# A delta-rule attention and expert kernel: 128 units written out with constant waits, and v brought into its bank by a transpose

## The chip, the cores and the metric

The kernel runs on one core of a Trainium2 chip. The metric is the time of one execution on the device in microseconds (us). A program on one core is timed several times; the time of before is the median of 3 runs.

## The reference, cut to what matters

The input has 4 sequences of 1024 tokens with 512 features. After a layer norm, 16 heads run a gated delta rule over time, and a mixture of experts follows. The change lies in the attention part:

```python
q = _short_conv(hidden_states @ Wq, conv_q)      # k and v likewise; silu at the end
q = _l2norm(q) * SCALE; k = _l2norm(k)
g_eff = -exp(A_log) * softplus(hidden_states @ Wf1 @ Wf2 + dt_bias)
beta = sigmoid(hidden_states @ Wb)
def step(S, inp):                                # for every token
    qt, kt, vt, gt, bt = inp
    S = S * exp(gt)[..., None]
    err = einsum('bhk,bhkv->bhv', kt, S)
    delta = bt[..., None] * (vt - err)
    S = S + kt[..., None] * delta[:, :, None, :]
    return S, einsum('bhk,bhkv->bhv', qt, S)
y = o * silu(hidden_states @ Wg + bg)            # then an RMS norm and Wo
```

## The kernel before, in words

The program has three parts. A prologue (to about 250 us) normalises x, transposes it into `xT`, and stores `beta` and the decays to scratch. The attention part (to about 5680 us) walks 128 units: 16 heads (H) times 8 chunks of 128 tokens (J), each unit holding all 4 sequences (B), 512 columns in all. The mixture (to the end) multiplies by Wo and runs the experts.

In the attention part a step works on three units at once. Unit a is being projected (q and k), convolved and normalised; unit m = a - 1 gets its table of decayed products between keys and queries in seven levels; unit b = a - 2 has its triangular system inverted in six levels and is scanned with the state. TensorE (PE), VectorE (DVE), ScalarE (ACT) and GpSimd (POOL) each have one `step` function, and the order of work in it is written out by hand. SyncE (SP) loads weights per head and `beta_u` and `decay_u` per unit. All engines meet only through semaphores, and each semaphore counts up by a fixed number per unit: `Signal.at(unit, k)` is the value that `wait` (L512) waits for.

`walk` calls `step` for each triple of units. It uses loops of the machine (`Fori`): an outer one over seven pairs of heads, in it an inner one per head over three pairs of chunks, and two steps written out at each head's end. The last two heads stand behind the outer loop and have only the inner one. Unit numbers are registers inside a loop, so that a wait's value and a DMA's address are computed by the engine's sequencer. In the last two steps of heads 14 and 15 they are constants.

What stands in a step around the seam between two steps: on PE, at the end, L839 (the state's update), L846 (transposes of keys), L852 (sums of squares of y) and L696 (transposes of the pairs); then in the next step `project(0)` (L660, 8 matmuls), `inverse_z(1)` (L708, which waits for `T_inv` from DVE), the diagonal (L672), `level(0)` (L686), `inverse_xt(1)` (L723, L727) and the first quarter of `project(1)` (L660), which waits for `gate`. On DVE: yg (L1009), the state (L1016, or a memset at a head's end, L1012), k_hat, q_hat, KR, KQ, `T_inv` (L939), then y_out (L1029). On ACT: the store of y_out (a DMA, L1178), then in the next step the table load and `gate` (L1094), `pre` (L1051), and the copies `take_t(1)` and `take_x(1)`.

In the middle of a step stands the block of the change, L805 and L806. PE brings v into bank 7 as rows of tokens, as the product of `v_u` with the identity, and adds the product of the decayed keys with the state. ACT copies the bank to `U_r` and `U_sb` (L1141, L1142). On PE `level(5)` (L686) follows directly. An f32 product of 128 columns is two passes in the trace, and an f32 transpose is one.

Of the kernel before, what the change touches and what calls it, by code (L numbers as in the profile page):

```python
# [52 lines left out]
def wait_apart(eng, sem, value, passed):  # L53

    eng.wait_ge(sem, value)
    eng.sem_inc(passed, 1)
# [44 lines left out]
def attention(nc, ctx, env):  # L101
# [7 lines left out]
    bank, ident, ones, ln_eps = env["bank"], env["ident"], env["ones"], env["ln_eps"]  # L109
# [4 lines left out]
    def sem(name):  # L114
        return ctx.enter_context(nc.semaphore(name))
# [20 lines left out]
    with ExitStack() as c0:  # L136
# [281 lines left out]
    v_u = sb("v_u", [P, UC])  # L418
# [24 lines left out]

    HEAD_LOADS = 8
    REFINEMENTS = 2
    dve_waits_passed, pool_waits_passed, sp_waits_passed = sem("dve_waits_passed"), sem("pool_waits_passed"), \
        sem("sp_waits_passed1")
    head_loaded = sem("head_loaded")
    unit_loaded = signal("unit_loaded", 32)
    y_stored = sem("y_stored")  # L450
# [24 lines left out]
    chunk_decay_ready = signal("chunk_decay_ready", 1)  # L475
# [3 lines left out]
    unit_ready = signal("unit_ready", 1)  # L479
# [29 lines left out]
    keys_scaled = signal("keys_scaled", LEVELS)  # L509

    def wait(eng, sig, unit, k):
        eng.wait_ge(sig.sem, sig.at(unit, k))  # L512

    def cols(b):
        return slice(b * P, (b + 1) * P)
# [21 lines left out]
    def walk(eng, step):  # L537


        step(Step(par_a=0, a=0, ja=0, a_first=True, odd=0))  # L540
        step(Step(par_a=0, a=1, ja=1, par_m=0, m=0, jm=0, m_first=True, odd=1))

        def head(h, par, last):
            with eng.Fori(0, J // 2 - 1) as jj:
                for odd in range(2):
                    j = eng.snap(jj * 2 + odd)
                    b = eng.snap(h * J + j)
                    step(Step(par_a=par, a=b + 2, ja=j + 2, par_m=par, m=b + 1, jm=j + 1, par_b=par, b=b, h=h, j=j, odd=odd))
            b = h * J + (J - 2) if isinstance(h, int) else eng.snap(h * J + (J - 2))
            if last:  # L550
                step(Step(par_m=par, m=b + 1, jm=J - 1, par_b=par, b=b, h=h, j=J - 2, odd=0))
                step(Step(par_b=par, b=b + 1, h=h, j=J - 1, ends=True, odd=1))
            else:
                step(Step(par_a=1 - par, a=b + 2, ja=0, a_first=True, par_m=par, m=b + 1, jm=J - 1, par_b=par, b=b, h=h,
                          j=J - 2, odd=0))
                b = b + 1 if isinstance(h, int) else eng.snap(h * J + (J - 1))
                step(Step(par_a=1 - par, a=b + 2, ja=1, par_m=1 - par, m=b + 1, jm=0, m_first=True, par_b=par, b=b, h=h,
                          j=J - 1, ends=True, odd=1))

        with eng.Fori(0, H // 2 - 1) as hp:  # L560
            for par in range(2):
                head(hp * 2 + par, par, False)
        head(H - 2, 0, False)
        head(H - 1, 1, True)

    block = ctx.enter_context(nc.Block())

    @block.sync
    def _(sp):
        def load_head(h, par):  # L570
            at = bass.ds(h * P, P)
            for m, W in enumerate((Wq, Wk, Wv, Wg)):
                sp.dma_start(weights[par][:, m, :, :], W.rearrange("(k p) n -> p k n", p=P)[:, :, at]) \
                    .then_inc(head_loaded, 16)
            for m, c in enumerate((conv_q, conv_k, conv_v)):
                sp.dma_start(taps[par][:, m, :], c[at, :]).then_inc(head_loaded, 16)
            sp.dma_start(bg_col[par][:], bg.rearrange("(c o) -> c o", o=1)[at, :]).then_inc(head_loaded, 16)

        def load_unit(h, j, odd):
            sp.dma_start(beta_u[:], beta_scratch[bass.ds(h, 1), bass.ds(j, 1), :].rearrange("a b c -> (a b) c")  # L580
                         .to_broadcast([P, UC])).then_inc(unit_loaded.sem, 16)
            rows = decay_scratch[bass.ds(h, 1), :, bass.ds(j, 1), :].rearrange("a g b c -> (a g) (b c)")
            sp.dma_start(decay_u[odd][:], rows.unsqueeze(1).to_broadcast([NG, GG, PC])).then_inc(unit_loaded.sem, 16)

        load_head(0, 0)
        load_unit(0, 0, 0)

        def buffers_free(u, first):
            wait_apart(sp, unit_ready.sem, unit_ready.at(u, 1), sp_waits_passed)
            if not first:  # L590
                wait_apart(sp, keys_scaled.sem, keys_scaled.at(u - 1, LEVELS), sp_waits_passed)
                wait_apart(sp, chunk_decay_ready.sem, chunk_decay_ready.at(u - 1, 1), sp_waits_passed)

        def head(h, par, last):
            first = isinstance(h, int) and h == 0
            start = 0
            if first:
                buffers_free(0, True)
                load_unit(0, 1, 1)
                buffers_free(1, False)  # L600
                load_unit(0, 2, 0)
                start = 1
            if start < J // 2 - 1:
                with sp.Fori(start, J // 2 - 1) as jj:
                    for odd in range(2):
                        j = sp.snap(jj * 2 + odd)
                        buffers_free(sp.snap(h * J + j), False)
                        load_unit(h, sp.snap(j + 1), 1 - odd)
            at = h * J if isinstance(h, int) else sp.snap(h * J)
            buffers_free(at + J - 2, False)  # L610
            load_unit(h, J - 1, 1)
            if not last:
                buffers_free(at + J - 1, False)
                load_unit(h + 1, 0, 0)

        def load_next(h, par):

            wait(sp, gate_ready, h * J - 1, 1)
            wait(sp, v_conv_steps, h * J - 1, TAPS - 1)
            load_head(h + 1, 1 - par)  # L620


        sp.wait_ge(head_loaded, 16 * HEAD_LOADS)
        load_head(1, 1)
        head(0, 0, False)
        with sp.Fori(0, H // 2 - 1) as hp:
            load_next(hp * 2 + 1, 1)
            head(hp * 2 + 1, 1, False)
            load_next(hp * 2 + 2, 0)
            head(hp * 2 + 2, 0, False)  # L630
        head(H - 1, 1, True)

    @block.tensor
    def _(pe):
        def step(s):
            a, m, b = s.a, s.m, s.b
# [163 lines left out]
            if b is not None:  # L800

                wait(pe, v_silu_ready, b, 1)
                wait(pe, scan_ready, b, 1)
                for i in range(B):
                    nc.tensor.matmul(bank[7][:, cols(i)], v_u[:, cols(i)], ident[:], start=True, stop=False)  # L805
                    last = nc.tensor.matmul(bank[7][:, cols(i)], KQ_scan[:, 0, cols(i)], state[:, cols(i)], start=False,  # L806
                                            stop=True)
                last.then_inc(u_done.sem, 1)
            level(5)
            inverse_xt(6)  # L810
# [813 lines left out]
```

## Time and profile before

| | us |
|---|---|
| median of 3 runs | 6507.95 (6507.94 to 6509.31) |
| the profiled execution | 6503.2 |
| its span, first to last instruction | 6501.5 |
| PE busy | 6114.4 |
| VectorE busy | 4381.3 |
| ScalarE busy | 2961.9 |
| GpSimd busy | 1768.7 |
| mean granted TensorE clock | 0.984 |

The page gives each engine's busy time and share. The timeline gives single instructions in order of time, neighbours of one line merged, with the idle time of the engine before them and what ended it in square brackets. "<-issue" is idle time in which the engine waited for nothing that the profile shows. PEld is PE's weight load and overlaps PE. Times count from the span's start.

### The profile page before, as it was taken

Reading aid. Unit: us, or ns where it says so; the run is one execution under the profiler, and the core shown is the slowest. Engines: PE = TensorE matmul, PEld = TensorE weight load, DVE = VectorE, ACT = ScalarE, POOL = GpSimd, SP = SyncE. Lnnn points to the kernel's source line nnn. Section 1 sums busy time; section 2 is a strip of 40 time slices with the busy share of each in tenths; the row PEclk is TensorE's granted clock in tenths of the full one; section 3 lists DMA queues with packets and bytes.
Section 4 is the critical chain, followed back from the end, with each engine's and each line's share of the span. In section 5 each row is a group of like instructions: output and inputs, shape, how many; then the busy total and the mean of one; then the engine's idle time right before and its main releaser. Section 6 shows DMA issues by size and latency. Waiting matters only on the chain. (4 is left out here: it accounts for less than half of the span.)

```text
span 6501.5 us, 107897 instructions
## 1 busy us (share of the span) xinstructions
PE 6114.4 (94%) x33720; PEld 4295.4 (66%) x33720; DVE 4381.3 (67%) x7563; ACT 2961.9 (46%) x5130; POOL 1768.7 (27%) x1636
## 2 busy tenths in 40 slices
PE   5699999999999999999999999999999999899999
PEld 2477777777777767776777777767777777644444
DVE  7677777777777777777777777777777777511110
ACT  2355545555555555554555555555555555401101
POOL 2233333333333333332333333333333333200000
PEclk8899999999999999999999999999999999899999
DMA  2101010101010110101010101000111100032221
GB/s 71 45 26 30 23 34 26 33 26 31 23 33 26 33 27 20 33 26 34 26 33 20 33 26 33 26 27 26 33 26 33 26 26 26 18 117 79 83 80 44
DMA packets 183586, 234.15 MB, mean 36 GB/s; under 512 B 25048, under 2 KB 128088, under 8 KB 179168
## 3 DMA queue, kind: packets, MB, share of 16 engines
q1 hardware_dynamic: 111072, 188.22, 9.9%
q10 hardware_dynamic: 72192, 41.95, 2.2%
q8 instruction: 164, 2.69, 0.2%
q14 instruction: 158, 1.29, 0.1%
HBM read 183.75 MB, written 46.38 MB: 35 GB/s over the span
## 5 line engine op out<-in xcount | busy, mean ns | idle before, releaser
L660 PE MATMUL bank<-xT,weights 128*128 (+1 forms) x4096 | 2176.9, 629 | 83.4 <-DMA bg_col<-in_L_attn_bg 34.2
L1196 POOL TENSOR_TENSOR KR<-KR,decay_u 128x256 f32<-128x256 f32 x896 | 920.2, 1027 | 2335.2 <-PE bank L686 2335.2
L903 DVE TENSOR_TENSOR KQ<-KQ,decay_u 128x512 f32<-128x512 f32 x896 | 626.0, 699 | 857.9 <-PE bank L686 857.7
L686 PEld LDWEIGHTS bank<-KQ,KR 128*128 128x128 f32 x7168 | 918.0, 191 | 248.8 <-issue 216.7
L888 DVE SCALAR_TENSOR_TENSOR conv<-pre,taps,conv 128x512 f32<-128x512 f32 x1152 | 917.1, 796 | 124.3 <-ACT conv L1067 110.7
L686 PE MATMUL bank<-KQ,KR 128*128 128x128 f32 x7168 | 953.6, 275 | 1.1 <-DVE KQ L903 0.7
L660 PEld LDWEIGHTS bank<-xT,weights 128*128 128x128 f32 x4096 | 657.7, 193 | 294.5 <-issue 214.9
L923 DVE COPY_PREDICATED all_pairs<-level_mask,bank 128x512 f32<-128x512 int32 x896 | 796.0, 888 | 0.0
L708 PEld LDWEIGHTS bank<-T_inv,pairs 128*128 128x128 f32 x3072 | 456.9, 193 | 468.5 <-issue 247.0
L708 PE MATMUL bank<-T_inv,pairs 128*128 128x64 f32 x3072 | 654.5, 338 | 61.1 <-DVE T_inv L939 59.5
L1111 ACT ACTIVATE T_inv<-bank 128x256 fp32r<-128x256 f32 x640 | 248.9, 389 | 635.2 <-PE bank L723 635.2
L727 PE MATMUL bank<-X,ZI 128*128 128x64 f32 x3072 | 472.8, 279 | 0.0
L1378 PE MATMUL bank<-wo,y_in 128*128 128x512 f32 x1024 | 447.9, 596 | 14.2 <-DMA wo<-in_L_attn_Wo 14.2
L1094 ACT ACT_TABLE_LOAD x128 | 164.2, 1283 | 588.3 <-DVE y_out L1029 391.1
L1222 POOL TENSOR_TENSOR X<-pairs,ident_each 128x512 fp32r<-128x512 f32 x128 | 182.0, 1422 | 868.3 <-PE bank L696 868.3
L727 PEld LDWEIGHTS bank<-X,ZI 128*128 128x128 f32 x3072 | 407.0, 193 | 0.0
L723 PE MATMUL bank<-ZI,X 128*128 128x64 f32 x2560 | 396.0, 281 | 3.0 <-DVE ZI L945 3.0
L1204 POOL TENSOR_TENSOR conv<-silu 128x512 f32<-128x512 f32 x256 | 266.4, 1041 | 443.9 <-ACT silu L1076 443.9
L945 DVE TENSOR_TENSOR ZI<-bank,ident_each 128x256 fp32r<-128x256 f32 x768 | 321.5, 419 | 89.2 <-PE bank L708 88.9
L931 DVE SCALAR_TENSOR_TENSOR pairs<-bank,level_mask 128x256 fp32r<-128x256 f32 x896 | 381.4, 426 | 0.0
L1208 POOL TENSOR_TENSOR squares_rest<-conv,squares 128x512 fp32r<-128x512 f32 x256 | 360.3, 1408 | 70.2 <-POOL conv L1204 70.2
L763 PEld LDWEIGHTS bank<-delta,pairs_scan 128*128 128x128 f32 x2048 | 248.6, 191 | 181.7 <-DVE delta L964 95.8
(162 smaller groups left out, 9128.9 us busy)
## 6 DMA issues: line engine op xcount, KB each, us to landing
decay_u<-decay_scratch SPq DMA_DIRECT2D x128, 510.0 KB
beta_u<-beta_scratch SPq DMA_DIRECT2D x128, 256.0 KB
y_scratch<-y_out ACTq DMA_DIRECT2D x128, 256.0 KB, 7.0
y_in<-y_scratch SPq DMA_DIRECT2D x32, 1024.0 KB, 4.8
xt<-in_L_attn_hidden_states SPq DMA_DIRECT2D x8, 1024.0 KB, 5.3
x_in<-in_L_attn_hidden_states SPq DMA_DIRECT2D x32, 256.0 KB, 5.1
out<-o_out ACTq DMA_DIRECT2D x32, 256.0 KB, 2.0
w<-in_L_ffn_W SPq DMA_DIRECT2D x8, 704.0 KB, 4.8
```

What stands on the lines that cost most here:

```text
L660: last = nc.tensor.matmul(bank[w % 2][:], weights[par][:, w, k, :], xT[:, k, bass.ds(j * UC, UC)], start=k == 0, stop=k == KC - 1)
L686: last = nc.tensor.matmul(to[:, :, i], KR[:, cols(i)], halves(KQ[:, :, cols(i)], l, 1), start=True, stop=True)
L708: last = nc.tensor.matmul(bank[5][:, half_cols(i)], pairs[:, l, cols(i)], halves(T_inv[:, cols(i)], l, 0), start=True, stop=True)
L723: last = nc.tensor.matmul(bank[7][:, half_cols(i)], X[:, cols(i)], halves(ZI[:, l - 1, cols(i)], l, 0), start=True, stop=True)
L727: last = nc.tensor.matmul(bank[6][:, half_cols(i)], ZI[:, l - 1, cols(i)], halves(X[:, cols(i)], l, 1), start=True, stop=True)
L888: nc.vector.scalar_tensor_tensor(conv[:, w], pre[:, w, :, t:t + P], taps[par][:, w, t:t + 1], conv[:, w], ALU.mult, ALU.add).then_inc(step ...
L903: nc.vector.tensor_tensor(second_halves, second_halves, pair[:, :, 0:1].unsqueeze(1).to_broadcast([P, 2, blocks, 1 << l]), ALU.mult).then_ ...
L923: nc.vector.copy_predicated(halves(all_pairs[:], l, 1), mask.bitcast(I32).unsqueeze(1).to_broadcast([P, 2, UC >> (l + 1), 1 << l]), src)
L931: nc.vector.scalar_tensor_tensor(halves(pairs[:, l], l, 1), src[:, 0], 1.0 / GRAIN, mask, ALU.mult, ALU.mult).then_inc(pairs_ready.sem, 1)
L1196: nc.gpsimd.tensor_tensor(first_halves, first_halves, second.to_broadcast([P, UC >> (l + 1), 1 << l]), ALU.mult).then_inc(keys_scaled.sem, 1)
L1208: nc.gpsimd.tensor_tensor(squares_rest[:, w], conv[:, w].rearrange("p b t -> p (b t)"), squares[:, w], ALU.subtract).then_inc(squares_rest ...
L1378: last = nc.tensor.matmul(bank[j % 2][:], y_in[j % 2][:, h, :], wo[:, h, :], start=h == 0, stop=h == H - 1)
```

## The change

`walk` calls `step` 130 times with plain numbers; no engine's program in the attention part has a loop, and every wait and address is a constant. SP's `buffers_free` and `head` become one list in the same order of loads and waits, without the semaphore increment behind each wait (`wait_apart`); DVE and POOL keep theirs. The product of v with the identity becomes PE's transpose, all four ahead of the products with the state; only the first one of the bank starts it.

```diff
@@ walk
-        def head(h, par, last):
-            with eng.Fori(0, J // 2 - 1) as jj:
-                for odd in range(2):
-                    j = eng.snap(jj * 2 + odd)
-                    b = eng.snap(h * J + j)
-                    step(Step(par_a=par, a=b + 2, ja=j + 2, par_m=par, m=b + 1, jm=j + 1, par_b=par, b=b, h=h, j=j, odd=odd))
...
-        with eng.Fori(0, H // 2 - 1) as hp:
-            for par in range(2):
-                head(hp * 2 + par, par, False)
-        head(H - 2, 0, False)
-        head(H - 1, 1, True)
+        for a in range(H * J + 2):
+            f = dict(odd=a % 2)
+            if a < H * J:
+                f.update(a=a, ja=a % J, par_a=a // J % 2, a_first=a % J == 0)
+            if 0 <= a - 1 < H * J:
+                m = a - 1
+                f.update(m=m, jm=m % J, par_m=m // J % 2, m_first=m % J == 0)
+            if a >= 2:
+                b = a - 2
+                f.update(b=b, h=b // J, j=b % J, par_b=b // J % 2, ends=b % J == J - 1)
+            step(Step(**f))
@@ SP
-        def buffers_free(u, first):
-            wait_apart(sp, unit_ready.sem, unit_ready.at(u, 1), sp_waits_passed)
-            if not first:
-                wait_apart(sp, keys_scaled.sem, keys_scaled.at(u - 1, LEVELS), sp_waits_passed)
-                wait_apart(sp, chunk_decay_ready.sem, chunk_decay_ready.at(u - 1, 1), sp_waits_passed)
...
+        for u in range(1, H * J):
+            h, j = u // J, u % J
+            if j == 1 and 1 <= h < H - 1:
+                load_next(h, h % 2)
+            wait(sp, unit_ready, u - 1, 1)
+            if u >= 2:
+                wait(sp, keys_scaled, u - 2, LEVELS)
+                wait(sp, chunk_decay_ready, u - 2, 1)
+            load_unit(h, j, u % 2)
@@ PE, in the middle of a step
                 for i in range(B):
-                    nc.tensor.matmul(bank[7][:, cols(i)], v_u[:, cols(i)], ident[:], start=True, stop=False)
+                    nc.tensor.matmul(bank[7][:, cols(i)], v_u[:, cols(i)], ident[:], is_transpose=True, start=i == 0,
+                                     stop=False, skip_group_check=True)
+                for i in range(B):
                     last = nc.tensor.matmul(bank[7][:, cols(i)], KQ_scan[:, 0, cols(i)], state[:, cols(i)], start=False,
-                                            stop=True)
+                                            stop=True, skip_group_check=True)
                 last.then_inc(u_done.sem, 1)
```

## Rows read from the trace of the kernel before

**Rows 1.** The page: busy time and share of PE, weight loads, DVE, ACT, POOL

```profile
PE 6114.4 (94%) x33720; PEld 4295.4 (66%) x33720; DVE 4381.3 (67%) x7563; ACT 2961.9 (46%) x5130; POOL 1768.7 (27%) x1636
```

**Rows 2.** PE's timeline, L839 of units 0, 48-50, 63, 64, 118-120, 126: start, length

```profile
303.72 1.06 PE L839 MATMUL bank<-delta,k_rows 128*128 128x128 f32 x8
...
2339.74 1.06 PE L839 MATMUL bank<-delta,k_rows 128*128 128x128 f32 x8
...
2381.68 1.06 PE L839 MATMUL bank<-delta,k_rows 128*128 128x128 f32 x8
...
2423.94 1.06 PE L839 MATMUL bank<-delta,k_rows 128*128 128x128 f32 x8
...
2969.62 1.06 PE L839 MATMUL bank<-delta,k_rows 128*128 128x128 f32 x8
...
3021.10 1.06 PE L839 MATMUL bank<-delta,k_rows 128*128 128x128 f32 x8
...
5303.01 1.06 PE L839 MATMUL bank<-delta,k_rows 128*128 128x128 f32 x8
...
5344.63 1.06 PE L839 MATMUL bank<-delta,k_rows 128*128 128x128 f32 x8
...
5385.98 1.06 PE L839 MATMUL bank<-delta,k_rows 128*128 128x128 f32 x8
...
5636.90 1.06 PE L839 MATMUL bank<-delta,k_rows 128*128 128x128 f32 x8
```

**Rows 3.** The timeline, all engines, a seam inside a loop

```profile
3028.25 0.74 DVE L1029 SCALAR_TENSOR_TENSOR y_out<-yg,norm_w_col,y_rn 128x512 f32<-128x512 f32 x1
...
3029.77 1.28 ACT L1094 ACT_TABLE_LOAD   x1 [4.34 <-DVE y_out L1029]
...
3031.81 0.30 PEld L660 LDWEIGHTS bank<-xT,weights 128*128 128x128 f32 x2 [0.21 <-ACT gate L1094]
```

**Rows 4.** The timeline, all engines, the seam behind unit 118, constants on both sides

```profile
5310.13 0.73 DVE L1029 SCALAR_TENSOR_TENSOR y_out<-yg,norm_w_col,y_rn 128x512 f32<-128x512 f32 x1
...
5310.26 0.64 PE L708 MATMUL bank<-T_inv,pairs 128*128 128x64 f32 x4 [0.47 <-DVE T_inv L939]
...
5311.32 1.28 ACT L1094 ACT_TABLE_LOAD   x1 [3.98 <-DVE y_out L1029]
...
5313.40 0.30 PEld L660 LDWEIGHTS bank<-xT,weights 128*128 128x128 f32 x2
```

**Rows 5.** The timeline, all engines, the seam with an outer branch, behind unit 63

```profile
2975.78 5.39 PE L660 MATMUL bank<-xT,weights 128*128 x8 [2.86 <-issue]
...
2984.80 1.28 ACT L1094 ACT_TABLE_LOAD   x1 [10.84 <-issue]
...
2986.83 2.07 PE L660 MATMUL bank<-xT,weights 128*128 x2 [2.59 <-ACT gate L1094]
```

**Rows 6.** Windows: stretch, length, busy (x instructions) per engine, granted clock, DMA share, GB/s

```profile
2987.00:2993.00 6.00, 6.00 (x17) 3.93 (x18) 0.42 (x1) 1.94 (x5) 0.00 (x0) 0.50 0.00 0
...
3021.00:3023.00 2.00, 1.69 (x16) 1.48 (x15) 1.91 (x6) 0.87 (x2) 0.00 (x0) 1.00 0.00 0
```

**Rows 7.** PE's timeline, the block of v and state; and transposes with products around them

```profile
3007.02 0.47 PE L805 MATMUL bank<-ident,v_u 128*128 128x128 f32 x2
...
3008.89 1.06 PE L686 MATMUL bank<-KQ,KR 128*128 128x128 f32 x8
...
5767.00 0.60 PE L1366 MATMUL bank<-ident,xn 128*128 128x128 f32 x4
5767.44 1.02 PE L1378 MATMUL bank<-wo,y_in 128*128 128x512 f32 x2
```

**Rows 8.** The timeline, DVE, POOL and ACT beside the block of v

```profile
3006.32 0.41 DVE L931 SCALAR_TENSOR_TENSOR pairs<-bank,level_mask 128x256 fp32r<-128x256 f32 x1
...
3007.56 1.40 POOL L1208 TENSOR_TENSOR squares_rest<-conv,squares 128x512 fp32r<-128x512 f32 x1 [0.27 <-POOL conv L1204]
...
3009.09 0.60 ACT L1141 ACTIVATE U_r<-bank 128x512 fp32r<-128x512 f32 x1 [2.79 <-PE bank L806]
```

More of the change, by code:

```diff
@@ L445, in attention @@
     REFINEMENTS = 2
-    dve_waits_passed, pool_waits_passed, sp_waits_passed = sem("dve_waits_passed"), sem("pool_waits_passed"), \
-        sem("sp_waits_passed1")
+    dve_waits_passed, pool_waits_passed = sem("dve_waits_passed"), sem("pool_waits_passed")
     head_loaded = sem("head_loaded")
@@ L537, in walk @@
     def walk(eng, step):
-        step(Step(par_a=0, a=0, ja=0, a_first=True, odd=0))
-        step(Step(par_a=0, a=1, ja=1, par_m=0, m=0, jm=0, m_first=True, odd=1))
-        def head(h, par, last):
-            with eng.Fori(0, J // 2 - 1) as jj:
-                for odd in range(2):
-                    j = eng.snap(jj * 2 + odd)
-                    b = eng.snap(h * J + j)
-                    step(Step(par_a=par, a=b + 2, ja=j + 2, par_m=par, m=b + 1, jm=j + 1, par_b=par, b=b, h=h, j=j, odd=odd))
[L549 to L558, printed above, removed]
-        with eng.Fori(0, H // 2 - 1) as hp:
-            for par in range(2):
-                head(hp * 2 + par, par, False)
-        head(H - 2, 0, False)
-        head(H - 1, 1, True)
+        for a in range(H * J + 2):
[9 more added lines that the diff above has]
+            step(Step(**f))
     block = ctx.enter_context(nc.Block())
@@ L583, in load_unit @@
             sp.dma_start(decay_u[odd][:], rows.unsqueeze(1).to_broadcast([NG, GG, PC])).then_inc(unit_loaded.sem, 16)
-        load_head(0, 0)
-        load_unit(0, 0, 0)
-        def buffers_free(u, first):
-            wait_apart(sp, unit_ready.sem, unit_ready.at(u, 1), sp_waits_passed)
-            if not first:
-                wait_apart(sp, keys_scaled.sem, keys_scaled.at(u - 1, LEVELS), sp_waits_passed)
-                wait_apart(sp, chunk_decay_ready.sem, chunk_decay_ready.at(u - 1, 1), sp_waits_passed)
[L594 to L614, printed above, removed]
         def load_next(h, par):
@@ L620, in load_next @@
             load_head(h + 1, 1 - par)
+        load_head(0, 0)
+        load_unit(0, 0, 0)
         sp.wait_ge(head_loaded, 16 * HEAD_LOADS)
         load_head(1, 1)
[L625 to L631, printed above, removed]
+        for u in range(1, H * J):
[7 more added lines that the diff above has]
+            load_unit(h, j, u % 2)
     @block.tensor
```

## The prediction

> **What bounds the kernel now.** I read the page first: TensorE (PE) is busy 94% of the span [rows 1], and the attention part with its 128 units holds 5.4 of the 6.5 ms. An average over the span hides what a unit waits for, so the next view is PE's timeline: the first matmul of L839 occurs once per unit, and the distance between two of them is one unit's period [rows 2]. Inside a loop body it is 41.94 us (2381.68 - 2339.74). Where the inner loop branches back in between it is 42.26 us (2423.94 - 2381.68). Where the outer loop branches back it is 51.48 us (3021.10 - 2969.62). One period lies in code without a loop and with constant waits on both sides, that from unit 118 to unit 119, in a head that the outer loop does not cover: 41.62 us (5344.63 - 5303.01). The one after it, a head's end, in which the state is cleared instead of updated, takes 41.35 us (5385.98 - 5344.63) although the next step starts a loop.
>
> Where do these differences arise? I laid the PE timelines of such periods on each other. They run alike but for one place, the seam between two steps. There PE's second projection (w = 1, L660) waits for `gate`, which ACT makes at the head of the new step, behind the store of `y_out`. In a loop ACT's table load starts 1.52 us after the start of L1029, and PE's weight load of L660 waits 0.21 us for the gate [rows 3]. In constant code the table load starts 1.19 us after L1029, and L660 waits for nothing [rows 4]. The 0.33 us between them is the register arithmetic for the store's address and the waits. With an outer branch, PE stands 2.86 us before the first L660 of the new step, ACT 10.84 us, and PE a further 2.59 us for ACT's gate [rows 5]. The clock granted to PE is 0.50, the lower of its levels (1.2 of 2.4 GHz), in the 6 us after that idle time [rows 6].
>
> So PE is the bound, but for the seam, where a chain through DVE and ACT ends last. What stays there is a wait of about 0.47 us for `T_inv` from DVE, which constant code has as well [rows 4].
>
> **The change, part by part.**
>
> *Loops and register waits of PE, DVE and ACT.* I price the whole of it by period, since each period shows its own cost. Units 0 to 126 are 126 periods, from 303.72 to 5636.90: 5333.2 us [rows 2]. Of them 15 end a head and 111 don't. In constant code I take 41.62 us for the 111, the one period that shows it, and 41.3 for the 15: the 41.35 measured has a loop's start behind it, and register arithmetic at that seam costs a little of the gate's slack. That is 111 x 41.62 + 15 x 41.3 = 5239.3 us, or 93.9 us less. The six outer branches hold between 6 x 5.4 (the two PE waits of [rows 5]) = 33 us and 6 x (51.48 - 41.3) = 61 us of it. The rest is 0.3 to 0.6 us in each ordinary period.
> Bounds of the whole: at the low end, the ordinary period only falls to the mean of in-loop periods without a branch (41.94), which leaves 5333.2 - 111 x 41.94 - 15 x 41.35 = 57.6 us. Above, the `T_inv` wait of 0.47 us goes too, 52 us more; nothing speaks for that, because constant code still has it, so I do not reach that far.
>
> *SP's queue.* The loads, their waits and their order stay: `load_next` stood before the load of a head's second chunk and still does. SP's loops and its semaphore increments go. They cost nothing now: no PE wait of the seam names a load of `beta_u` or `decay_u` [rows 3 to 5]. If that cover were gone, the cost would be that of one load's delay at a seam, and the edit makes SP no later. POOL keeps its increments; it is idle for much of each unit.
>
> *v by transpose.* Per unit, 8 passes of a 128-column f32 product with the identity (L805; each f32 product is two passes) become 4 single-pass transposes. In the run now, 16 passes of L805 and L806 take from 3007.02 to 3008.89, 1.87 us or 0.117 each; after the first pass the spacing is about 0.112 [rows 7]. Four f32 transposes of the same form (L1366, data as weights and the identity moving) take from 5767.00 to 5767.44, and the next product starts right behind: 0.44 us, 0.11 each [rows 7]. So 8 x 0.112 - 4 x 0.11 = 0.45 us goes in each unit, and 128 x 0.45 = 58 us in all. The new order, all transposes ahead of the products with `state`, adds no wait and no pass. That a product accumulates behind a transpose in the same bank is not in the trace. As bounds I take nothing extra, and half a pass (0.05 us) at the switch, 6 us; the switch from L1366 to L1378 shows nothing, so I take nothing.
> What follows must be early enough for all of it to count. `level(5)` comes next on PE, at 3008.89. Its input from DVE (L931) is ready at 6.32 + 0.41 = 3006.73 [rows 8], 2.2 us before, and its input from POOL stands ahead of L1208 in POOL's order. POOL ends L1208 at 3008.96 and then waits for `level(5)`, which ends at 3009.95 [rows 7, 8]. ACT waits 2.79 us for the block of v [rows 8]. So all that follows waits for PE or for something that did, and the unit's later part moves by 0.45 us as a whole. Next late would be POOL: its slack of 1.0 us falls to 0.5.
>
> *The sum.* 94 + 58 = 152 us. The profiled execution took 6503.2 us (span 6501.5), so 6351 us is forecast for such a one. The median of the runs shown is 6507.95, 4.7 us above it; I put the forecast against the median: 6507.95 - 152 = 6356 us.
>
> **A rule against the change, weighed.** In the trace the unit already has four f32 transposes (L846), and the stretch around them runs at a granted clock of 1.00 [rows 6]. The Trainium skill, "TensorE: Matmul & The Clock Gate", Part 4: PE-mode transpose, says that transposes do not count as PE-busy in the way that products do. By that rule four more of them could bring the clock down, and the time would be that of rival 5 below instead of 6356; the trace does not bear it out, with 1.00 around L846.
>
> **The rivals.**
> 1. *Both parts pay, as above*: 6356 us, 84%.
> 2. *Constants pay only at branches.* Something else, such as the DVE chain to `T_inv`, ends last at most seams, and unit 118's 41.62 is not typical. Then the loops give the 57.6 us of the lower bound: 6508 - 58 - 58 = 6392 us, 6%. For it: only one period in the trace is free of registers. Against it: its seam differs from the others in just the 0.33 us on ACT that has a cause.
> 3. *The transposes pay nothing*, because a chain beside PE fills the 0.45 us, or the pass is no cheaper here: 6508 - 94 = 6414 us, 4%. Against it stand the slacks of [rows 8]. That the program does not do what it says, and emits products as before, has the same time.
> 4. *Slower: straight code starves PE.* Each unit's instructions now are new, whereas the inner loop's body is reused three times. If each of the 128 units met one stall like PE's at the outer branch (2.86 us [rows 5]), that would be 366 us: 6508 - 152 + 366 = 6722 us. It turns the sign from 1.2 us per unit (152/128). Against it: the steps at each head's end are straight code in the run now, and the periods there (41.62 and 41.35 us [rows 2]) hold no such stall. 4%.
> 5. *Slower: the clock.* If the additional transposes bring the clock down for a stretch like the 6 us of [rows 6], half of that is lost, 3 us per unit, 384 us in all: 6740 us. It decides from 1.2 us per unit as well. 2%, since the clock stays at 1.00 around L846 [rows 6].
>
> **How the numbers follow.** Case 1 alone holds 84%, with an own range of 6343 to 6370: 0.1 us per unit either way is 13 us. I stretch the upper end to 6385 toward case 2, since an ordinary period that falls only halfway between 41.94 and 41.62 gives 18 us more. The low end is 6340. Faster by over 0.2% (13 us, about what a measurement of this kernel can tell from no change): 0.94; within: 0.01; slower: 0.05.
>
> **What would show it.** In the new trace the distance between L839's first matmuls should be about 41.17 us (41.62 - 0.45) in ordinary units and 40.85 at head ends, with no 50 us period and no PE wait from issue at L660. The transposes should be 4 per unit, and the block from the first of them to the next `level(5)` should take about 1.4 us in place of 1.87. Table loads should start about 1.2 us after L1029, the `T_inv` wait should stay near 0.47, and the mean granted clock should rise above 0.984. The prediction is wrong if PE shows waits from issue spread evenly over the units, if the clock falls in the middle of units, or if the 0.45 us returns as a PE wait for ACT or POOL behind the block.

## The result, and the profile after

| | before | after |
|---|---|---|
| median of 4 runs, us | 6508.63 (6507.94 to 6509.42) | 6359.36 (6355.84 to 6360.9) |
| the profiled execution | 6503.2 | 6360.9 |
| its span | 6501.5 | 6359.2 |
| instructions in the span | 107897 | 92850 |
| mean granted clock | 0.984 | 0.984 |

After takes 0.977 of before's time, with a 95% interval of 0.9753 to 0.9787: 149 us less, where 152 were forecast.

The page of after, busy times first, then two of its DMA queues. The columns are those of [rows 1]; of a queue, its packets, megabytes and share of the 16 engines:

```profile
PE 6024.0 (95%) x33208; PEld 4223.0 (66%) x33208; DVE 4372.9 (69%) x7563; ACT 2959.6 (47%) x5130; POOL 1765.8 (28%) x1636
...
q8 instruction: 268, 4.39, 0.3%
q14 instruction: 181, 1.48, 0.1%
```

PE has 33720 - 33208 = 512 matmuls fewer than in [rows 1], the 4 passes per unit that the transposes save. What the page doesn't show is the unit, so here is PE's timeline of after: the first matmul of the state's update, which is L798 now (L839 before), of units 0, 56 to 58, 63 and 64. It answers to [rows 2]:

```profile
306.90 1.06 PE L798 MATMUL bank<-delta,k_rows 128*128 128x128 f32 x8
...
2649.85 1.06 PE L798 MATMUL bank<-delta,k_rows 128*128 128x128 f32 x8
...
2690.99 1.06 PE L798 MATMUL bank<-delta,k_rows 128*128 128x128 f32 x8
...
2896.70 1.06 PE L798 MATMUL bank<-delta,k_rows 128*128 128x128 f32 x8
...
2937.46 1.06 PE L798 MATMUL bank<-delta,k_rows 128*128 128x128 f32 x8
```

An ordinary period is 41.14 us (2690.99 - 2649.85). The one behind unit 63, which took 51.48 before, is a head's end like any other now, with 40.76 us (2937.46 - 2896.70).

The seam between two steps, in the timeline of after, behind unit 57. It answers to [rows 3] and [rows 4]; L665 is the old L708, L617 the old L660, L1053 the gate:

```profile
2656.37 0.68 DVE L898 TENSOR_TENSOR T_inv<-bank,ident_each 128x512 fp32r<-128x512 f32 x1
2656.97 0.74 DVE L988 SCALAR_TENSOR_TENSOR y_out<-yg,norm_w_col,y_rn 128x512 f32<-128x512 f32 x1
...
2657.11 0.64 PE L665 MATMUL bank<-T_inv,pairs 128*128 128x64 f32 x4 [0.47 <-DVE T_inv L898]
2657.74 0.37 ACTq L1137 DMA_DIRECT2D y_scratch<-y_out  x1
2658.14 1.28 ACT L1053 ACT_TABLE_LOAD   x1 [3.96 <-DVE y_out L988]
...
2660.24 0.30 PEld L617 LDWEIGHTS bank<-xT,weights 128*128 128x128 f32 x2
```

The table load starts 1.17 us behind the start of y_out, as in constant code before (1.19) and not as in a loop (1.52). PE's second projection waits for nothing. The wait for `T_inv` is the same 0.47 us.

The block of v, PE's timeline of after; it answers to [rows 7]:

```profile
5478.95 0.66 PE L762 MATMUL bank<-ident,v_u 128*128 128x128 f32 x4
5479.44 1.06 PE L765 MATMUL bank<-state,KQ_scan 128*128 128x128 f32 x8
5480.33 1.06 PE L643 MATMUL bank<-KQ,KR 128*128 128x128 f32 x8
```

From the first transpose to `level(5)` it takes 1.38 us, where it took 1.87: 0.49 us less per unit. The clock around it, in windows of after over a whole ordinary unit and over the beginning of a step (columns as in [rows 6]), is the full one of 2.4 GHz:

```profile
2649.00:2690.00 41.00, 39.63 (x243) 29.53 (x243) 31.88 (x57) 21.91 (x39) 13.39 (x12) 1.00 0.10 27
...
2904.00:2910.00 6.00, 6.00 (x44) 5.04 (x43) 3.92 (x9) 4.14 (x7) 1.26 (x1) 1.00 0.64 172
```

**The balance of the two profiled executions.** Units 0 to 125 took 5291.8 us before (5595.49 - 303.72) and take 5138.4 us (5445.34 - 306.90): 153.4 less. The first state update comes 3.2 us later (306.90 against 303.72), and from unit 125's update to the end after takes 7.8 us longer (913.8 against 906.0). The sum is -153.4 + 3.2 + 7.8 = -142.4 us, the difference of the two spans (-142.3) but for rounding. The medians differ by 149 because the profiled execution of before is 5.4 us under its median and that of after 1.5 us over its own. The last two terms are taken up in the section on why the prediction was right; the experiments look at the first.

### The profile page after: what moved, and what is told of

It reads as the page before. It is cut to its first block and busy times, and to the rows that moved or that the text cites. A ratio compares the mean times of both kernels' runs of the same rounds, so it can differ in the third digit from the quotient of the medians.

```text
span 6359.2 us, 92850 instructions
## 1 busy us (share of the span) xinstructions
PE 6024.0 (95%) x33208; PEld 4223.0 (66%) x33208; DVE 4372.9 (69%) x7563; ACT 2959.6 (47%) x5130; POOL 1765.8 (28%) x1636
## 3 DMA queue, kind: packets, MB, share of 16 engines
q1 hardware_dynamic: 111072, 188.22, 10.2%
## 5 line engine op out<-in xcount | busy, mean ns | idle before, releaser
L617 PE MATMUL bank<-xT,weights 128*128 128x512 f32 x4096 | 2160.0, 625 | 36.7 <-DMA bg_col<-in_L_attn_bg 36.7
L617 PEld LDWEIGHTS bank<-xT,weights 128*128 128x128 f32 x4096 | 654.6, 192 | 228.5 <-issue 190.5
L665 PEld LDWEIGHTS bank<-T_inv,pairs 128*128 128x128 f32 x3072 | 456.2, 192 | 468.3 <-issue 243.6
L665 PE MATMUL bank<-T_inv,pairs 128*128 128x64 f32 x3072 | 660.3, 340 | 60.3 <-DVE T_inv L898 57.6
L1337 PEld LDWEIGHTS bank<-wo,y_in 128*128 128x128 f32 x1024 | 193.0, 191 | 248.6 <-issue 248.4
```

Of the source, the lines that this page charges most:

```text
L617: last = nc.tensor.matmul(bank[w % 2][:], weights[par][:, w, k, :], xT[:, k, bass.ds(j * UC, UC)], start=k == 0, stop=k == KC - 1)
L665: last = nc.tensor.matmul(bank[5][:, half_cols(i)], pairs[:, l, cols(i)], halves(T_inv[:, cols(i)], l, 0), start=True, stop=True)
L1337: last = nc.tensor.matmul(bank[j % 2][:], y_in[j % 2][:, h, :], wo[:, h, :], start=h == 0, stop=h == H - 1)
```

## The experiments

All times are medians of four runs of a kernel, its ratio against the runs of before that were timed beside it (medians 6503.29 to 6504.92 us). After itself was timed beside a before of 6508.63, some 4 us more, so a few us between a run's time and after's say nothing; where it matters the text goes by the periods, which agree to 0.1 us where the attention part's code is equivalent (5138.4 and 5138.4 us in after and in the interleaved run). In the first group each part of the change is done alone or undone alone. "Units 0 to 125" is the distance of the first matmuls of their state updates in the kernel's one profile, as above; it leaves out prologue, last units and mixture, and so scatters less than the whole time.

### The two parts, each alone

Only the block of v, in the loops of before:

```diff
                 for i in range(B):
-                    nc.tensor.matmul(bank[7][:, cols(i)], v_u[:, cols(i)], ident[:], start=True, stop=False)
+                    nc.tensor.matmul(bank[7][:, cols(i)], v_u[:, cols(i)], ident[:], is_transpose=True, start=i == 0,
+                                     stop=False, skip_group_check=True)
+                for i in range(B):
                     last = nc.tensor.matmul(bank[7][:, cols(i)], KQ_scan[:, 0, cols(i)], state[:, cols(i)], start=False,
```

> The kernel before with only the block of v changed to transposes; all loops stay. My theory, that the block is on PE's path in every unit and all that follows waits for PE: each period 0.45 us shorter (41.94 to 41.49 in a loop without a branch, 42.26 to 41.81 with one), 128 x 0.45 = 58 us, 6450 us. Rival, that the gate at the next seam takes the gain in a loop: periods unchanged, 6508 us. The seam's own waits (0.21 us for the gate, about 0.5 for T_inv) should stay as they are.

Measured: 6444.71 us (6439.75 to 6448.69), ratio 0.9909 (0.9893 to 0.9926), 58.6 us less than before. Units 0 to 125 take 5228.3 us, 63.5 less: 0.48 us in each ordinary period, and 6.2 us in the six with an outer branch together.

Only the program without loops, with the old block of v in it (the edit is against after):

```diff
-                    nc.tensor.matmul(bank[7][:, cols(i)], v_u[:, cols(i)], ident[:], is_transpose=True, start=i == 0,
-                                     stop=False, skip_group_check=True)
-                for i in range(B):
+                    nc.tensor.matmul(bank[7][:, cols(i)], v_u[:, cols(i)], ident[:], start=True, stop=False)
```

> The changed kernel with the product with the identity put back; no loops, constant waits. Theory: what the changed kernel took plus 0.45 us per unit: ordinary period 41.59 (41.14 + 0.45), head end 41.22, total 6359 + 58 = 6417 us. Rival, that the two parts share a gain (each alone gives more than its share): below 6400 or above 6430 us.

Measured: 6421.86 us (6411.81 to 6426.15), ratio 0.9869 (0.9852 to 0.9885), 81.4 us less. Units 0 to 125 take 5199.4 us, 92.4 less, with an ordinary period of 41.63 and a head's end of 41.25.

The two parts add: 63.5 + 92.4 = 155.9 us in these units, and both together give 153.4. So neither takes the other's place, and a chain that hides one of them (rivals 2 and 3) isn't there. The span of the second is only 77.1 us shorter than that of before, 15.3 less than its units say: its start came 3.8 us later (307.50 against 303.72), and what follows unit 125 took 11.6 us longer, 6.3 of them in the period to unit 126 (47.68 against 41.41), of which more below.

### Which loop costs how much

The outer loop alone written out, the inner loops of three passes kept (against after; SP as in after):

```diff
-        with eng.Fori(0, H // 2 - 1) as hp:
-            for par in range(2):
-                head(hp * 2 + par, par, False)
-        head(H - 2, 0, False)
+        for h in range(H - 1):
+            head(h, h % 2, False)
         head(H - 1, 1, True)
```

> The changed kernel, but each head has its inner loop over three pairs of chunks again on PE, DVE, ACT and POOL; only the outer loop is gone. Theory: every head goes like head 14 of the kernel before (334.3 us) less 8 x 0.45, that is 330.7 us against 328.8: 6359 + 16 x 1.9 = 6390 us, no period over 42. Rival, that nearly all of the loops' cost was the six outer branches: 6360 us. Rival, that each entry into an inner loop behind new code stalls PE as the outer branch did (some 3 us and more a head): 6359 + 30 + 48 = 6437 us or more.

Measured: 6380.18 us (6379.06 to 6389.01), ratio 0.9814 (0.9797 to 0.983). Units 0 to 125 take 5167.3 us. Its ordinary periods are 41.26 us inside a body, 41.66 over an inner branch, 41.40 where the inner loop is left, and 40.86 at a head's end: a head's eight periods are 330.7 us, as the theory has them, and neither rival holds. The time is 10 us under the 6390 forecast because what follows unit 125 is 9.1 us shorter than in after (904.7 against 913.8). A list of waits, PE's part, sum in us, times, longest:

```profile
PE bank L629 <- ACT gate L1065: 10.5, 33, 0.6
```

So of the loops' price in these units, 5228.3 - 5138.4 = 89.9 us beside the transposes, 61.0 us (5228.3 - 5167.3) go with the outer loop and 28.9 us (5167.3 - 5138.4) with the inner ones. The outer loop's part is again two: its six branches, whose periods with the transposes alone are 46.93 to 49.78 us, 290.9 together, cost 290.9 - 6 x 40.86 = 45.7 us, and the other 15 us lie in the ordinary periods (41.43 with head numbers in registers, 41.26 without). PE waits for `gate` 33 times in this run and never in after.

### Which engine's loops cost

After, with one engine's walk put back into the loops of before, the other engines straight. The edit for ACT:

```diff
-        walk(act, step)
+        walk_in_loops(act, step)
```

where `walk_in_loops` is the `walk` of the kernel before.

> The changed kernel, but ACT alone walks in the loops of before; PE, DVE, POOL and SP have no loops. Theory, that ACT's register arithmetic and branches between y_out and gate make the ordinary periods' loss: 41.49 in a loop, 41.8 with an inner branch; ACT's 10.8 us stall at an outer branch also comes back in large part, some 5 us of each of the six: 111 x 0.43 + 30 = 78 us, 6437 us. Rival, that PE's own arithmetic is what costs: 6360 us.

Measured: 6455.02 us (6451.92 to 6460.94), ratio 0.9927 (0.991 to 0.9943), 95.7 us slower than after. Units 0 to 125 take 5234.7 us. The timeline behind unit 63, where ACT takes the outer branch, and the list of waits:

```profile
2957.06 1.28 ACT L1082 ACT_TABLE_LOAD   x1 [9.97 <-issue]
...
2959.09 2.08 PE L646 MATMUL bank<-xT,weights 128*128 128x512 f32 x2 [6.12 <-ACT gate L1082]
```

```profile
PE bank L646 <- ACT gate L1082: 52.3, 46, 6.7
```

ACT alone costs 5234.7 - 5138.4 = 96.3 us, all that the loops cost and a little more. Behind unit 63 ACT is idle for 9.97 us; 3.6 us of such idle time, for y_out, it has at this seam in after too, so the branch holds it up for 6.4. PE waits 6.12 us for its gate and then runs at a granted clock of 0.61 (window 2959:2967), and the period is 50.04 instead of 40.76 us. The six such periods are 299.7 us together, 55.2 over 6 x 40.76, or 9.2 each where I had expected some 5; that is the miss in the forecast of 6437 us. The other 41 us are spread over the seams in loops: 41.40 us inside a body and 41.76 over an inner branch, against 41.15.

The same edit for PE:

```diff
-        walk(pe, step)
+        walk_in_loops(pe, step)
```

> The changed kernel, but PE alone walks in the loops of before; ACT, DVE, POOL and SP have no loops. With ACT alone in loops the periods came to 41.40, 41.76 and 50 us. Theory, that PE's own registers and inner branches lie behind its queue and cost nothing, and its outer branch costs its stall of 2.9 us and little else: ordinary periods 41.14, outer ones 40.77 + 3 to 5, so 6359 + 6 x 4 = 6383 us. Rival, that ACT's and PE's costs overlap in the kernel before, so that either alone brings back all: 6440 us or more.

Measured: 6379.73 us (6376.99 to 6382.08), ratio 0.9812 (0.9795 to 0.9828), 20.4 us slower than after. Units 0 to 125 take 5165.4 us, 27.0 more. PE's timeline behind unit 63:

```profile
2910.36 1.06 PE L827 MATMUL bank<-delta,k_rows 128*128 128x128 f32 x8
...
2916.61 5.39 PE L646 MATMUL bank<-xT,weights 128*128 x8 [2.95 <-issue]
...
2955.62 1.06 PE L827 MATMUL bank<-delta,k_rows 128*128 128x128 f32 x8
```

The period is 45.26 instead of 40.76 us. Of these 4.5 us, 2.95 are the stand, and the most of the rest is the clock: the eight matmuls of L646 take 5.39 us instead of the 3.65 that they take in after (L617), as the clock granted is 0.70 in the window 2916.7:2922.3. The six such periods are 271.7 us together, 27.1 over 6 x 40.76, which is all of it: the ordinary periods are 41.14 us even over an inner branch. An inner branch and the register waits cost PE nothing that shows; they cost ACT. The medians show 20.4 and not 27.0 us because what follows unit 125 is 9.9 us shorter here than in after (903.9 against 913.8).

The same for DVE:

```diff
-        walk(dve, step)
+        walk_in_loops(dve, step)
```

> The changed kernel, but DVE alone walks in the loops of before. With ACT alone the ordinary periods came back to 41.40 and 41.76 and the outer ones to 50, with PE alone they stayed at 41.14, and the outer ones were 45.3. Theory, that DVE's chain at the seam runs behind its queue and only its branches show: ordinary 41.14 to 41.2, under 0.4 more with an inner branch, under 3 at an outer one: 6359 + 10 to 30 us. Rival, that DVE's register arithmetic is on the path to T_inv as ACT's is on the path to the gate: 41.3 and more in every period, 6359 + 30 us and more.

Measured: 6358.75 us (6355.69 to 6364.68), ratio 0.9778 (0.9761 to 0.9796), after's time. Its periods are 41.175 and 40.79 us, 0.02 to 0.03 us over those of after (41.155 and 40.76), and its outer branches show nothing in the periods. DVE has 69% of the span busy, yet its register arithmetic lies in gaps. POOL's loops and SP's were not put back alone; ACT's and PE's leave nothing for them to explain.

### The order of transposes and products

Transpose i directly ahead of product i, all in one loop of four:

```diff
                 for i in range(B):
                     nc.tensor.matmul(bank[7][:, cols(i)], v_u[:, cols(i)], ident[:], is_transpose=True, start=i == 0,
                                      stop=False, skip_group_check=True)
-                for i in range(B):
                     last = nc.tensor.matmul(bank[7][:, cols(i)], KQ_scan[:, 0, cols(i)], state[:, cols(i)], start=False,
```

> The changed kernel with each transpose ahead of its own product with the state (v of sequence i, then state of sequence i), as in the order of before, in place of four transposes and then four products. Theory, that the switch between transpose and product costs nothing: block 1.38 us, period 41.14, 6359 us. Rival, that each switch costs about 0.05 us: 7 switches in place of 1, period 41.4, 6397 us.

Measured: 6359.44 us (6353.4 to 6360.75), ratio 0.9773 (0.9756 to 0.9791), with an ordinary period of 41.153 us. PE's timeline of the block:

```profile
2676.61 0.33 PE L762 MATMUL bank<-ident,v_u 128*128 128x128 f32 x1
2676.78 0.39 PE L764 MATMUL bank<-state,KQ_scan 128*128 128x128 f32 x2
2677.00 0.27 PE L762 MATMUL bank<-ident,v_u 128*128 128x128 f32 x1
...
2678.00 1.06 PE L643 MATMUL bank<-KQ,KR 128*128 128x128 f32 x8
```

The block takes 1.39 us with seven switches between transpose and product as with one (1.38). A transpose takes 0.11 us to the next matmul (2677.00 to 2677.11 in its successor), a pass of a product the same. The switch that I had bounded with half a pass costs nothing that shows.

### What is left at the seam

The runs above leave one wait at the seam, 0.47 us for `T_inv`. Three edits of after ask what it hides. First, DVE makes `T_inv` directly behind KR, ahead of the two KQ that the next unit needs:

```diff
                 nc.vector.tensor_tensor(KR[:], k_hat[:], beta_u[:], ALU.mult)
+                first_inverse()
...
-            first_inverse()
+            if a is None:
+                first_inverse()
```

> The changed kernel with T_inv (DVE) made before the two KQ operations instead of behind them. PE's wait of 0.47 us for T_inv goes, and PE waits for KQ less than 0.1 us instead. Theory, that the gate on ACT is next late, with a slack of under 0.1 us: PE's projection then waits some 0.4 us for the gate, and the period falls by only 0.05: 6354 us. Rival, that the gate has room: ordinary periods 40.7, 6312 us.

Measured: 6339.53 us (6339.02 to 6341.69), ratio 0.975 (0.9734 to 0.9766), 19.8 us under after. Its ordinary period is 41.07 us, its head's end 40.40. PE's waits:

```profile
PE bank L617 <- ACT gate L1055: 20.3, 109, 0.5
PE bank L665 <- DVE T_inv L898: 3.5, 2, 2.8
```

The wait for `T_inv` is gone (57.6 us in after) and a wait for the gate is in its place 109 times: of 0.47 us per ordinary unit only 0.08 is kept: two waits stand behind one another, and the shorter one hides behind the longer. At a head's end, where DVE has less to do and y_out comes early, 0.36 us is kept. I had expected nothing there and was wrong. These periods hold 110 x 0.08 + 15 x 0.36 = 14 us. The two profiled executions are 21.9 us apart; of the other 8, 2.4 are an earlier first update and 5.5 lie behind unit 125 (its period is 39.74 here and 47.20 in after), of which more below.

Second, the store of y_out, for which ACT waits ahead of its gate, is issued in the next step behind gate and `pre` (`store_unit(u)` is the wait and the DMA taken out below, for unit u; the last one stands behind `walk`):

```diff
             silu_gate()
             take_projection(0)
+            if b is not None and b >= 1:
+                store_unit(b - 1)
             take_t(1)
...
-                wait(act, y_ready, b, 1)
-                act.dma_start(y_scratch[...], by_batch(y_out[:])).then_inc(y_stored, 16)
```

> The changed kernel with ACT's store of y_out issued in the next step, behind the table load, the gate and the first projection's copy, instead of ahead of them. The gate is then ready some 2 us earlier. Theory, that nobody waits for it in constant code: period unchanged at 41.14, 6359 us. Rival, that the gate is what ends last at the seam: 6310 us or so.

Measured: 6356.09 us (6352.82 to 6359.81), ratio 0.9776 (0.976 to 0.9793), and 41.14 and 40.77 us as in after. ACT's table load starts 2.8 us ahead of y_out (2650.67 against 2653.45) where in after it stands 1.2 us behind, and nobody was waiting for it. The timeline has `T_inv`'s wait where it was:

```profile
2653.58 0.64 PE L665 MATMUL bank<-T_inv,pairs 128*128 128x64 f32 x4 [0.47 <-DVE T_inv L898]
```

Third, both:

> Both at once: T_inv before KQ on DVE, and the store behind the gate on ACT. Theory, that the two chains end within 0.1 us of each other and only both together move PE: ordinary periods 41.14 - 0.42 = 40.72, head ends unchanged at 40.77, 111 x 0.42 = 47 us: 6312 us. Rival, that a third chain (KQ to the diagonal, or the copies on ACT behind the store) is as late: under 10 us gained, 6350 us.

Measured: 6298.93 us (6294.84 to 6300.0), ratio 0.9687 (0.9671 to 0.9703), 60.4 us under after, with periods of 40.69 and 40.40. Alone the edits bring 13.9 and 0.3 us in units 0 to 125, together 110 x 0.46 + 15 x 0.36 = 56. I had expected the head's ends unchanged at 40.77, and missed their 0.36. PE's list of waits names the gate no more, and `T_inv` twice, 3.5 us in all.

In its timeline the seam shows one thing more:

```profile
2626.55 1.37 POOL L1189 TENSOR_TENSOR X<-pairs,ident_each 128x512 fp32r<-128x512 f32 x1 [6.80 <-PE bank L653]
2626.82 1.65 DVE L937 TENSOR_TENSOR KR<-k_hat,beta_u 128x512 f32<-128x512 f32 x1
...
2629.29 0.94 PE L665 MATMUL bank<-T_inv,pairs 128*128 128x64 f32 x4
...
2630.33 1.16 PE L629 MATMUL bank<-q_hat,KR 128*128 128x128 f32 x8
```

DVE's KR, with POOL's X beside it, takes 1.65 us. PE's diagonal (L629), which needs the last KQ, starts 1.04 us behind L665. The last edit lets POOL's X wait until DVE has made both KQ:

```diff
+            if s.a is not None:
+                wait_apart(pool, unit_ready.sem, unit_ready.at(s.a, 1), pool_waits_passed)
```

> T_inv ahead of KQ and the store behind the gate, as in the fastest kernel so far (6299 us, ordinary period 40.69, head ends 40.40), and POOL's X = pairs + identity additionally waits until DVE has made KQ. Beside POOL's 1.4 us operation one DVE operation (KR) takes 1.64 us in place of 0.69. Theory, that this 0.95 us is the last wait of the seam (PE's diagonal for KQ): ordinary periods fall to the head ends' 40.40, 111 x 0.29 = 32 us: 6267 us. Rival, that X is then late for inverse_xt(1), or that y_out suffers in KR's place and matters: 6299 us or more.

Measured: 6265.44 us (6261.31 to 6269.84), ratio 0.9634 (0.9617 to 0.9651). Ordinary periods are 40.40 us, as head's ends:

```profile
2612.66 0.69 DVE L937 TENSOR_TENSOR KR<-k_hat,beta_u 128x512 f32<-128x512 f32 x1
...
2615.13 0.94 PE L665 MATMUL bank<-T_inv,pairs 128*128 128x64 f32 x4
2615.33 1.61 POOL L1191 TENSOR_TENSOR X<-pairs,ident_each 128x512 fp32r<-128x512 f32 x1 [9.74 <-DVE KQ L943]
2615.89 1.14 PE L629 MATMUL bank<-q_hat,KR 128*128 128x128 f32 x8
```

KR takes 0.69 us without X beside it, and the diagonal follows 0.76 us behind L665 instead of 1.04: these 0.28 us are the difference of the periods (40.69 - 40.40 = 0.29). This version is the fastest here, 239 us under the before timed beside it; its units 0 to 125 take 88.2 us less than after's (5050.2 against 5138.4).

## Why the prediction was right, and where it wasn't

**The loops: right in size and in mechanism.** I had 93.9 us for 126 periods from a single constant period of 41.62 us and an end of 41.3. The program without loops and with the old block has 41.63 and 41.25, and its 125 periods to unit 125 are 92.4 us under before's. Rival 2, that unit 118 was not typical, falls with it. The place is ACT's seam, as read in [rows 3, 4]: ACT in loops costs all of it, PE in loops only its stand at the outer branch and the clock behind it, and DVE 0.02 to 0.03 us a period. The 10.84 us of ACT in [rows 5] that the prediction calls its stand hold some 4 us in which ACT waits for y_out at a head's end without a branch as well (3.99 us behind unit 7).

**The outer branch.** I bounded the six of them between 33 and 61 us, from one of them. All six periods of before are 46.60 to 51.47 us, 297.1 together, which is 49 us over 6 x 41.3; the one that I read is the longest. The lower end had only PE's two waits of [rows 5]; the part that was missing in it is the lower clock behind each of them. A window over the first projection of before, 2975.8:2981.3, has a granted clock of 0.69 (0.70 with PE in loops), and its eight matmuls take 1.7 us longer, of which 1.1 reach the next instruction (L708, 4.83 us behind their start, where it is 3.74 in straight code). Behind the wait for the gate the clock is 0.50 [rows 6]. PE's timeline there, of before and, at the same place, of the straight code with the old block:

```profile
2980.61 0.94 PE L708 MATMUL bank<-T_inv,pairs 128*128 128x64 f32 x4
...
2986.83 2.07 PE L660 MATMUL bank<-xT,weights 128*128 x2 [2.59 <-ACT gate L1094]
...
2993.86 1.10 PE L660 MATMUL bank<-xT,weights 128*128 x2
```

```profile
2931.15 3.65 PE L617 MATMUL bank<-xT,weights 128*128 128x512 f32 x8
2934.89 0.64 PE L665 MATMUL bank<-T_inv,pairs 128*128 128x64 f32 x4
...
2938.06 1.10 PE L617 MATMUL bank<-xT,weights 128*128 128x512 f32 x2
...
2942.03 1.10 PE L617 MATMUL bank<-xT,weights 128*128 128x512 f32 x2
```

One round takes 7.03 us against 3.97, 3.1 more, which is the larger part of the clock's price. Waits and clock together are 5.45 + 1.1 + 3.1 = 9.6 of the 10.2 us that this period has over a head's end. The costs of PE's and ACT's stands don't add: 27 us for PE alone and 55 for ACT alone, but 46 for all engines together, with the transposes in each.

**The transposes: right, a little under-sized.** 0.45 us per unit was the term, 0.49 is measured on the block, and 63.5 / 125 = 0.51 on the periods, where 0.48 is the ordinary one's and the six with an outer branch scatter. My spacing of a pass was 0.112; the sixteen passes as a whole had 0.117 [rows 7], and the twelve that stay take 0.115 each (1.38 us). The 0.49 us pass to the unit's end as a whole, as the slacks of [rows 8] said, and POOL's reduced slack shows nowhere.

**The rivals on the slow side.** Straight code doesn't starve PE: L617 has no wait from issue, and the six of before (18.1 us together, [rows 5] is one) are gone. The four f32 transposes leave the clock alone, with 1.00 over a whole unit. The Trainium skill, "TensorE: Matmul & The Clock Gate", Part 4: PE-mode transpose, says that they don't count as PE-busy as products do; among the products of this kernel it had no effect that a row shows.

**The wait for T_inv** stayed at 0.47 us (57.6 us over 112 times), so the upper bound that took it away too was rightly left out. What the prediction didn't ask is what stands behind it; the runs on the seam show that it was the gate, then DVE's KR held up by POOL's X.

**What the sum left out.** Two terms that I had at nothing are +3.2 and +7.8 us in the profiled pair. The first is the wait of the first projection for the load of `bg_col`, 34.2 us before and 36.7 after. It is 36.5 with the transposes alone, in the loops of before, and 34.5 in the straight code with both seam edits, so it doesn't follow the change; these are 2.5 of the 3.2 us. The second lies in the last steps, where no new unit's q and k are projected and PE has nothing to do while DVE makes `T_inv`. PE's timeline of before, then of after:

```profile
5595.49 1.06 PE L839 MATMUL bank<-delta,k_rows 128*128 128x128 f32 x8
...
5602.76 1.06 PE L708 MATMUL bank<-T_inv,pairs 128*128 128x64 f32 x4 [3.98 <-DVE T_inv L939]
5603.64 2.05 PE L672 MATMUL bank<-q_hat,KR 128*128 128x128 f32 x8
...
5607.05 0.95 PE L723 MATMUL bank<-ZI,X 128*128 128x64 f32 x4
```

```profile
5445.34 1.06 PE L798 MATMUL bank<-delta,k_rows 128*128 128x128 f32 x8
...
5452.59 1.06 PE L665 MATMUL bank<-T_inv,pairs 128*128 128x64 f32 x4 [3.95 <-DVE T_inv L898]
5453.47 2.05 PE L629 MATMUL bank<-q_hat,KR 128*128 128x128 f32 x8
...
5469.68 2.05 PE L617 MATMUL bank<-xT,weights 128*128 128x512 f32 x2
5471.53 1.51 PE L643 MATMUL bank<-KQ,KR 128*128 128x128 f32 x8
```

Both stand 4 us, and behind it the clock is 0.50. Eight matmuls of L629 take 2.05 us instead of 1.14. In before the full clock is back at about 5607, after 4 us; in after at about 5471, after 18 us. The windows over it:

```profile
5603.00:5607.00 4.00, 4.00 (x20) 4.00 (x21) 1.60 (x4) 1.97 (x2) 0.00 (x0) 0.50 0.21 66
```

```profile
5453.00:5470.00 17.00, 17.00 (x75) 15.97 (x75) 8.36 (x16) 4.81 (x9) 3.48 (x3) 0.50 0.06 16
```

So this period took 41.41 us before and 47.20 after, 5.8 of the 7.8 us; 1.8 more lie in the next one (39.45 and 41.23). The long period doesn't come from straight code as such: over all kernels of the study it took either 38.9 to 41.4 us or 47.2 to 47.7, with loops (47.35 with ACT's, 41.03 with all, 40.28 with PE's) and without (47.17 interleaved, 40.88 with the store later). Each kernel has one profile, so whether one kernel meets both values from run to run was not seen. What decides it stays open.

**The mean granted clock** stayed at 0.984, against my statement that it would rise. The trace's clock, summed up as us lost against the full one, says why. Over units 0 to 125 it is 22.2 us in before and nothing in after, so the branches' low stretches did go, and that alone would have made 0.987. But the last two periods lost 27.2 us instead of 17.2, and the prologue 59.7 instead of 52.9 (58.0 in each of the other eleven kernels). The whole is 99.0 us of 6359 against 104.1 of 6501. The mean of a whole execution was a poor test, since stretches outside the units change it as much as the six branches do; the clock of units 0 to 125 would have been a good one.

**Where luck helped.** The two terms for the units came out at 153.4 us, 3 more than the periods of the prediction give for them (150.3), and 11 us that it had at nothing stood against them in the profiled pair. That the medians then differ by 149, so near 152, owes something to before's profiled execution, 5.4 us under its median.

**Five periods of after are longer** than 41.15 by 0.1 to 0.4 us (units 19, 33, 67, 83, 94), 1.3 us together, and four or five at the same units in three other kernels without loops. They may be the loading of code; no run tests it.

## What to carry to other kernels

Take a period of one step in each kind of code that the trace has, lay them on each other, and price a change by the differences: the one constant period of before gave the loops' price to within 2 us of 92. Ask for each engine alone what its registers and branches hold up; here registers and inner branches cost nothing on PE, next to nothing on DVE and 41 us on ACT, which is 46% busy but issues late what PE wants early; an outer branch cost 4.5 us with PE alone in loops and 9.2 with ACT alone. And where one wait at a seam hides another, remove both before judging either: alone 13.9 and 0.3 us, together 56.

## What the runs showed of the hardware

- The price of a taken branch differs by engine and by distance. At the six outer branches PE stood 2.8 to 3.3 us (before, and with PE alone in loops). ACT was idle 9.0 to 11.2 us in before and 9.8 to 10.6 with ACT alone in loops; less the 4.0 us that it waits at such a seam without a branch, that is 5.0 to 7.2 and 5.8 to 6.6. DVE's next instruction came 0.34 us late behind unit 63. At the inner branch of the same loops PE lost nothing and a period with ACT in loops 0.36 us (41.76 against 41.40). The Trainium skill, "Runtime: NRT & Kernel Launch", section "Instruction fetch mechanics", says that a branch to code which isn't loaded has to fetch it first and that sequential code is fetched ahead. The trace agrees as far as it goes: no wait from issue at L617 in after, though the instruction queue q8 carries 268 packets in place of 164, and in before PE stood at the far branch alone. That the stands are a fetch no run shows, nor why ACT pays about twice what PE does.
- A stand of PE can cost twice, once in itself and once at the lower clock behind it: at the outer branch of before 2.86 us and 1.1 behind it, then 2.59 and 3.1. How long the lower clock lasts was not the same behind equal stands: 4 us in before and 18 in after, behind 3.98 and 3.95 us at the end of the attention part.
- Transposes and products in f32 alternate in one bank at no cost that shows (1.39 us for the block with seven switches, 1.38 with one), 0.11 us a pass either way, and the product adds to what the transpose left there.
- A DVE operation on two operands in SBUF waited for one of POOL's beside it. KR took 1.65 us beside X and 0.69 without; X ended at 2627.92 and KR 0.55 us later, at 2628.47. The Trainium skill, "SBUF — State Buffer", section "SBUF: two separate sides", says that such a pair shares a port and the later one blocks for the whole of the other. The trace agrees, and it turned a POOL operation that nobody waited for into 0.28 us on each of 110 units.
